# Second layer's routing written out batch by batch and worked in two lots, with its normalisation on three engines

## The reference

```python
xf = layernorm(x)                       # per token, 4096 tokens
scores = sigmoid(xf @ gate_w + bias)    # 128 -> 8
top_scores, top_idx = top_k(scores, 2)
top_scores /= sum(top_scores) + 1e-6
w = zeros(T, 8).at[arange(T), top_idx].add(top_scores)
up = einsum('th,ehi->tei', xf, up_w) + up_b
eo = einsum('tei,eih->teh', gelu(up), down_w) + down_b
combined = einsum('teh,te->th', eo * 0.1, w)
shared = (gelu(xf @ sw_up + sb_up) @ sw_down + sb_down) * 0.1
out = shared + combined
out = out / (max(abs(out)) + 1e-6)
x = x + out
```

## Time and profile before

| | us |
|---|---|
| median of 3 runs | 988.51 (987.65 to 989.19) |
| profiled execution, time | 990.38 |
| profiled execution, span | 988.6 |
| start of the stage `route` in it (ACT's first instruction) | 671.04 |
| first matmul of the stage behind it | 723.19 |

### The profile page before, as it was taken

The page is one execution under the profiler, slowest core; times in us unless marked ns, Lnnn a source line. Parts: engine busy times, 40 slices in busy tenths (PEclk is TensorE's granted clock), DMA queues, the critical chain, the costliest instruction groups (busy, mean ns, idle before and its releaser), DMA issues. The chain is left out here.

```text
span 988.6 us, 18788 instructions
## 1 busy us (share of the span) xinstructions
PE 808.0 (82%) x5585; PEld 601.9 (61%) x5585; DVE 637.7 (65%) x1445; ACT 503.9 (51%) x1081; POOL 417.4 (42%) x520
## 2 busy tenths in 40 slices
PE   2798816898159899999999999977278899999993
PEld 2566606898125456565555656546236899999862
DVE  4578643558729987777777777727721566568457
ACT  3475423565114566767767676664122366665520
POOL 3664567547277113232332332221167720273174
PEclk9999857999669999999999999995579899999997
DMA  5920014544144121313122131000012222242222
GB/s 156 366 81 1 30 47 137 160 141 138 30 149 134 44 84 43 99 32 99 44 96 76 51 99 46 17 1 0 6 48 72 94 80 75 81 116 76 78 61 69
DMA packets 82155, 80.45 MB, mean 81 GB/s; under 512 B 9856, under 2 KB 61758, under 8 KB 82110
## 3 DMA queue, kind: packets, MB, share of 16 engines
q1 hardware_dynamic: 73122, 62.68, 20.8%
q0 software_dynamic: 8192, 16.79, 5.8%
q10 hardware_dynamic: 796, 0.42, 0.2%
HBM read 41.06 MB, written 38.80 MB: 81 GB/s over the span
## 5 line engine op out<-in xcount | busy, mean ns | idle before, releaser
L1619 ACT ACTIVATE Pb<-ps,low 128x512 f32<-128x512 f32 x320 | 216.3, 688 | 134.0 <-PE ps L1718 87.6
L902 POOL DMA_INDIRECT YG<-yslots,slot x128 | 131.3, 1026 | 149.3 <-DMA yslots<-yb 78.9
L1497 DVE TENSOR_REDUCE m<-ps 128x4 f32<-128x1024 f32 x128 | 156.3, 1222 | 54.1 <-PE ps L1695 35.9
L1718 PE MATMUL ps<-Q,KZ 128*128 128x128 f32 (+3 forms) x512 | 172.2, 398 | 4.8 <-ACT Pb L1619 4.0
L390 POOL DMA_INDIRECT xslots<-XN,slot x128 | 124.0, 969 | 72.2 <-issue 37.5
L1421 POOL TENSOR_SCALAR_AFFINE_SELECT Pb<-Pb 128x512 f32<-128x512 f32 (+1 forms) x84 | 67.6, 804 | 190.8 <-ACT Pb L1619 190.2
L1263 PE MATMUL ps<-xT,wst 128*128 128x128 f32 x960 | 137.4, 282 | 7.8 <-DVE wst L1132 5.0
L1718 PEld LDWEIGHTS ps<-Q,KZ 128*128 128x128 f32 x512 | 93.1, 192 | 81.8 <-ACT Pb L1619 56.1
L1275 PE MATMUL ps<-wst,hb 128*128 128x128 f32 x960 | 134.0, 277 | 6.6 <-ACT hb L1082 6.1
L1085 ACT ACTIVATE hb<-ps,upb 128x128 f32<-128x128 f32 x320 | 91.3, 368 | 76.6 <-PE ps L1263 76.6
L1263 PEld LDWEIGHTS ps<-xT,wst 128*128 128x128 f32 x960 | 123.6, 198 | 9.5 <-DVE wst L1132 6.1
(11 more groups left out here) (256 smaller groups left out, 1239.9 us busy)
## 6 DMA issues: line engine op xcount, KB each, us to landing
xt<-xslots SPq DMA_DIRECT2D x40, 256.0 KB
yslots<-yb SPq DMA_DIRECT2D x40, 256.0 KB, 2.3
terms<-high SPq DMA_DIRECT2D x32, 256.0 KB, 2.2
Q<-terms SPq DMA_DIRECT2D x128, 48.0 KB
KZ<-terms SPq DMA_DIRECT2D x128, 48.0 KB
xslots<-YG SPq DMA_DIRECT2D x2, 2560.0 KB, 11.8
terms<-low SPq DMA_DIRECT2D x16, 256.0 KB, 2.3
X<-in_L_attn_x_dram SPq DMA_DIRECT2D x4, 512.0 KB, 6.0
```

What stands on the lines that cost most here:

```text
L902: pool.indirect_dma_start(out=s.YG[:, TB * w + j, k, :], out_offset=None, in_=s.yslots[group][:, :], in_offset=bass.IndirectOffsetOnAxis(a ...
L1497: w = dve.tensor_reduce(top[:, :, (TB + 1, 3, TB, None, 1)[u]], ps.rearrange("p (t g k) -> p g t k", t=2, g=HG), AX.XY, ALU.max)
L1619: act.activation(Pb[:, NCH * (gg % 2) + c, :], bank(4 + c % 2), ACT.Exp, bias=s.low[:, :], scale=DH ** -0.5)\
L1718: w = pe.matmul(ps[:, col:col + T - kt * P], KZ[:, HG * gg + g, kt * P:kt * P + P], Q2[gg % 2][:, kt * P:T], start=True, stop=not masked)
```

## The change

The stage `route` is rewritten; nothing else is, except that all later line numbers grow by 28.

- The loops are written out, so no instruction takes a register for its address.
- The rows are normalised from X straight into XN. Of each of the first four batches DVE does two tiles, ACT one and POOL one; of each of the last four ACT does two, POOL two and DVE none. ACT needs the shift -mean/std, one new DVE instruction over all tiles. The copies to nb and XN are gone.
- PE transposes XN, ACT writes the result straight to xf, and `logits` reads xf. POOL's copy is gone.
- DVE selects lot 0 as soon as batches 0 to 3 have logits, reads batches 4 and 5, then reads the ranks and places lot 0, then reads batches 6 and 7, selects lot 1, computes lot 0's gates, places lot 1 and computes lot 1's gates. Copies and gates that covered 32 tiles in one instruction cover 16 in each of two.
- PE's `rank` of lot 0 stands behind the logits of batch 5.
- POOL's memset of the gates stands behind its 12 normalisations, and ROUTE_TILES is 5 (10 scatters in this stage, not 6).

```diff
-ROUTE_TILES = 3
+ROUTE_TILES = 5
...
+    def rows_of(b):
+        first = TB * b
+        if b < GD:
+            return range(first, first + 2), range(first + 2, first + 3), range(first + 3, first + 4)
+        return range(0), range(first, first + 2), range(first + 2, first + 4)
...
+            scales(dve, s, 3)
+            dve.scalar_tensor_tensor(shift[:, :], s.mv[:, :, 0], -1.0, s.rstd[:, :], ALU.mult, ALU.mult).then_inc(by_dve, 1)
+            for b in range(GD):
+                norm(b)
+            for b in range(GD):
+                logits(b)
+            select(0)
+            logits(GD)
+            logits(GD + 1)
             read_rank(dve, s, 0, psR[0], 1)
-            dve.wait_ge(s.mb_ready, 2 * NG)
-            for k in two:
-                link(dve.tensor_copy(s.wg[:, k, :, :], s.hot[:, k, :, :]))
             place(dve, s, link, 0, 1)
-            dve.nop().then_inc(exp_in, 1)
...
+            for b in range(GD + 2, B):
+                logits(b)
+            select(1)
+            gates(0)
             read_rank(dve, s, 1, psR[1], 1)
             place(dve, s, link, 1, 1)
+            gates(1)
...
+            act.wait_ge(by_dve, 1)
+            norm(0)
+            for b in range(B):
+                if b + 1 < B:
+                    norm(b + 1)
+                evacuate(b)
...
+            pool.wait_ge(s.stats_sems[3], STDS[3] + 1)
+            for b in range(B):
+                for j in rows_of(b)[2]:
+                    w = pool.tensor_scalar(s.XN[:, j, :], s.X[:, j, :], s.mv[:, j, 0:1], s.rstd[:, j:j + 1], ALU.subtract, ALU.mult)
+                w.then_inc(by_pool, 1)
+            pool.memset(s.gate9[:, :, :], 1.0).then_inc(by_pool, 1)
             scatter(pool, s, 0, 0, ROUTE_TILES, 1)
...
+            turn(0)
+            for b in range(B):
+                if b + 1 < B:
+                    turn(b + 1)
+                logits(b)
+                if b == GD + 1:
+                    rank(pe, s, 0, psR[0], 1)
+            rank(pe, s, 1, psR[1], 1)
```

More of the change, by code:

```diff
@@ L791, in _ @@
[L791 to L802, removed]
@@ L803, in _, with norm, logits, select @@
-            for g in range(NG):
+            link = Links(dve, chain)
+            def norm(b):
+                for j in rows_of(b)[0]:
+                    w = dve.tensor_scalar(s.XN[:, j, :], s.X[:, j, :], s.mv[:, j, 0:1], s.rstd[:, j:j + 1], ALU.subtract, ALU.mult)
+                w.then_inc(by_dve, 1)
+            def logits(b):
+                dve.wait_ge(logit_ready, b + 1)
+                dve.tensor_copy(s.L[:, TB * b:TB * b + TB, :], psL[b % 2]).then_inc(logit_read, 1)
+            def select(g):
+                count = TB * GROUPS[g]
+                L = s.L[:, tiles_of(g), :]
+                dve.wait_ge(logit_read, FIRST[g] + GROUPS[g])
+                link(dve.tensor_tensor(L, L, s.bcast[:, 2 * P:2 * P + E].unsqueeze(1).broadcast_to([P, count, E]), ALU.add))
@@ L826, in _ @@
         def _(act):
-            act.sem_inc(xn_ready, 2)
-            scale_roots(act, s, 3)
-            with act.Fori(0, B // 2) as i:
-                for k in two:
-                    b = 2 * i + k
-                    act.wait_ge(nb_ready, b + 1)
-                    act.activation(s.XN[:, bass.ds(TB * b, TB), :], nb[k][:, :, :], ACT.Identity).then_inc(xn_ready, 1)
-                    act.wait_ge(turned, b + 3)
-                    act.wait_ge(xf_done, b + 1)
-                    act.activation(xs[k][:, :], psT[k], ACT.Identity).then_inc(xs_ready, 1)
@@ L837, in _, with norm, evacuate @@
-            act.wait_ge(exp_in, 2)
-            top = s.top[:, 0:2, :]
-            act.activation(top, top, ACT.Sigmoid).then_inc(exp_ready, 1)
+            def norm(b):
+                for j in rows_of(b)[1]:
+                    w = act.activation(s.XN[:, j, :], s.X[:, j, :], ACT.Identity, bias=shift[:, j:j + 1], scale=s.rstd[:, j:j + 1])
+                w.then_inc(by_act, 1)
+            def evacuate(b):
+                act.wait_ge(turned, b + 1)
+                act.activation(s.xf[:, T * b:T * b + T], psT[b % 2], ACT.Identity).then_inc(xf_ready, 1)
@@ L841, in _ @@
+            scale_roots(act, s, 3)
+            act.wait_ge(by_dve, 1)
[4 more added lines that the diff above has]
+                evacuate(b)
+            for g in range(NG):
+                act.wait_ge(exp_in, 2 + g)
+                top = s.top[:, 0:2, tiles_of(g)]
+                act.activation(top, top, ACT.Sigmoid).then_inc(exp_ready, 1)
         @block.gpsimd
         def _(pool):
-            pool.sem_inc(xf_done, 2)
```

78 lines of the change are left out of this document (37 added, 41 removed).

## The result

The changed kernel takes 979.65 us (median of 4 runs, 978.14 to 980.79), the kernel before, run beside it, 988.85 (987.65 to 990.58). The ratio is 0.990 with a 95% interval of 0.987 to 0.992: faster by 8 to 13 us. The forecast was 980.1 with a range of 977.8 to 984.2. The profiled execution took 980.71, its span is 979.0.

The account below looks back on a forecast made before the run. The stage was held by PE's batches, then by DVE's chain behind them. Ending it at 714.8 instead of 723.19 (-8.4) takes the profiled 990.38 to 982.0; the median, 988.51 before, becomes 980.1, range 977.8 to 984.2.

Parts of the forecast that it names:

- The sum: Stage end: DVE done at 713.9, then 0.1 and 0.77 to the shared expert's first matmul, 714.8 for 723.19: -8.4 us.
- Start: Stage's beginning: normalising on three engines lets PE's first transposes start at 674.2 (bounds 674.0 to 674.8), before at 674.85.
- Pace: PE's batches of transposes and logits: 2.6 us each at half clock, not below 2.55, in place of 2.66.
- Lot 0: DVE under PE's batches: from batch 3's logits at 686.0, selection, ranks and placing end at 698.0 instead of 712.61.
- Behind it: DVE after placing lot 0: last logits, lot 1's selection and placing, both lots' gates, 15.9 us, ending at 713.9.
- POOL: Stage's end: ten scatters take 12.5 us, the drain 1.5 more, ending at 712.9, one us below DVE.
- the partial gain: Rival, stage's end: scatters stretch (+1.8), shift blocked (+0.6), gates in halves cost as whole (+1.6); together 984; chance 0.12.
- The clock: Rival, PE's batches: TensorE's clock rises to 2.4 GHz, a batch costs some 1.4 us, time 975.6; chance 0.06.
- POOL's tiles decide: Rival, normalising: POOL's 12 tiles take far over 0.8 us each; at 3.0 the time is 993.7; chance 0.05.
- The point where the gain is gone (2.4): POOL's normalising: at about 2.4 us a tile, late last logits use up the whole gain.
- the threshold below it: POOL's normalising: up to 1.7 us a tile nothing is lost; beyond, each 0.1 costs 1.2 on the last logits.

Follow-up runs that it names:

- the tiles: The changed kernel with ROUTE_TILES 7 in place of 5, so 14 scatters in the stage and not 10: 982.92 us, 0.994 of before.
- the doubled kernel: The changed kernel with each of POOL's 12 tiles normalised once more into a tile nobody reads: 983.46 us, 0.993 of before.
- the tripled kernel: The changed kernel with each of POOL's 12 tiles normalised twice more into a buffer nobody reads: 990.59 us, 1.000 of before.
- the kernel with the 30 added ones: 30 unread bf16 512-column matmuls before PE ranks lot 1, added to the kernel with gates and lot 1's placing in the next block: 970.56 us, 0.981 of before.
- the gates late: The changed kernel with both lots' gates computed in the next block, still 5 tiles scattered in the stage: 980.23 us, 0.990 of before.

## Why the prediction was right

*The sum.* The stage was forecast at 41.7 and is 41.52, and the rest stayed, within what it varies by of itself (0.56 longer, where two profiles of one kernel differ by 2.7). That the median came within 0.5 of the forecast is in part luck, since the head moves by up to 4.7 and the rest by 2.7 from profile to profile. That the mechanism is the overlap and not the normalising is shown by the kernel without it (stage 50.00). The kernel with the old normalising (46.98) shows what the prediction does not price: the overlap needs the shared-out normalising to free DVE. That DVE's chain and not POOL ends the stage is shown by the tiles (3.4 more for four scatters, after 1.6 of cover) and by moving gates away.

*Start.* 1.10 as forecast (1.1). The shift was not blocked by POOL: it took 0.19 and started 0.07 ahead of POOL's first tile.

*Pace.* The forecast took 2.6 a batch and held that it could not be below 2.55, from 0.72 and 1.83 of loads. It is 2.45. Timeline of after, PE's loads:

```profile
678.35 0.90 PEld L889 LDWEIGHTS ps<-ident,XN 128*128 128x128 f32 x4
679.23 1.83 PEld L897 LDWEIGHTS ps<-gateW,xf 128*128 128x128 f32 x8
680.80 0.90 PEld L889 LDWEIGHTS ps<-ident,XN 128*128 128x128 f32 x4
```

The group of line 897 ends at 681.06, behind the start of the next one at 680.80. Lengths of groups that overlap don't add up to a bound. It made the forecast of batch 3's logits 0.6 late, to the good. The prediction also put the loops' removal at no more than 0.06 a batch. The kernel with the old normalising has the loops written out too and reads a batch's logits every 2.45 (at 6.06, 8.52, 10.97 and 13.42), so the 0.2 gained on 2.66 does not come from sharing out the normalising; whether the loops or POOL's vanished copy to xf gave it, no run separates.

*Lot 0.* From there to placing 12.2 was forecast and 12.07 measured. The ranks cost no wait on either side, with 0.05 between the selection and PE in place of the forecast's 0.3: whatever makes the selection later is paid, as the doubled kernel shows.

*Behind it.* 15.9 was forecast and 16.3 measured. The gates in halves take 1.9 (701.34 to 703.24), as chosen between 1.4 and 2.77. What was missed: the two copies at line 808 take 0.65, not 0.45, and gates of lot 1, which come straight behind placing, first wait 0.49 for its last write. With 0.1 more from DVE's end to the first matmul, that took back most of what the pace gave.

*POOL.* Ten scatters take 12.7 (12.5) and the drain 1.7 more (1.5). Placing to the first scatter is 0.3 in place of 0.86. Cover below DVE: 1.6 (1.0). They did not stretch beside DVE: eight took 0.96 at most as before, the first 1.22 (1.11 before) and one 1.06.

*The rivals.* Of the partial gain's three costs the scatters' and the shift's did not come, and of the gates' 1.6 only 0.4, as the wait of 0.49 for the last write. The clock did not rise: PE was busy 5.00 of 5 us twice over at 0.50. The Trainium skill ("TensorE: Matmul & The Clock Gate", "What's actually happening") says that activity releases the throttle; here 26 matmuls in 5 us, all of them fp32 transposes of 128 columns and matmuls of 8, did not, and two bf16 matmuls of 512 columns a batch, behind seven at the start, did. That POOL's tiles decide was rightly held unlikely at 0.80. The point where the gain is gone (2.4) came out, by luck: the prediction had the last logits come late behind a placing that stays, and in the tripled kernel PE waits before batch 6's transposes and placing itself moves by 9.5. The step that was wrong outright is the threshold below it: nothing lost up to 1.7. It counted POOL's last tile only; the first ones are late before that (1.4), and POOL's work beside DVE's selection costs DVE too (1.0).

## What to carry to other kernels

Where one engine's loop is followed by another's chain, look for the part of the chain that needs only half of the loop's results; what it takes is to free the chain's engine of its share in the loop, or the overlap brings a third. Before moving work under such an overlap, write down for each engine when it reaches the barrier, drain included, since the second-latest caps what can be gained; and ask what on the chain is needed behind the barrier at all, which here was worth more than the change itself. A slow supplier is to be judged at its first delivery as well as at its last.

## What the runs showed of the hardware

- TensorE's granted clock stayed at 0.50 (1.2 GHz) while PE was busy 15.00 of 15 us with transposes and 8-column matmuls (675 to 690 of the kernel with the 30 added ones), and rose to 1.00 (2.4 GHz) when 512-column matmuls were added.
- Behind a wait TensorE's same first matmuls take more or less from profile to profile, by how late the clock rises: the shared expert's first eight 5.26 to 6.68, with the clock over 715 to 720 at 0.88 and at 0.59 in two profiles of one kernel, and the experts' first 24 4.54 to 5.46. All the rest behind the stage repeats within 0.5 in 249.
- Some of DVE's instructions with two inputs take 0.40 to 0.52 in place of 0.29 beside POOL's normalising: five of nine in the doubled kernel, one (0.40) and the last (0.83 for 0.69) in the tripled one. The first layer's pair in which DVE's took 1.25 had two inputs on both engines.
- The drain of POOL's indirect transfers at a block's end ends 1.4 to 1.9 us behind the last scatter, and it, not the scatters' end, is what the others wait for: where POOL is last, PE's first matmul comes 0.7 to 0.8 behind the drain (716.3 and 717.01 with seven tiles, 713.5 and 714.17 with the gates late).
